# The output head of an S4 + recurrent-cell kernel: seven products for eight from stored row sums, two tiles at a time, with the state's term seeded in PSUM and the residual sum on GpSimd

## The chip, the cores and the metric

The kernel runs on one core of one Trainium2 chip. The metric is the device time of one execution in microseconds (us). Five engines work side by side: TensorE (PE, with its weight loads as PEld), VectorE (DVE), ScalarE (ACT), GpSimd (POOL) and SyncE (SP), which here only issues transfers. They synchronise by semaphores that the program writes out by hand.

## What is computed

Input x has 8 sequences of 2048 steps with 512 channels. A first layer normalises, convolves each channel with a long kernel and adds its normalised result back (the stored `x1`). The second layer normalises x1 to x2, runs a gated cell over 8 blocks of 2048 rows in 4 chains, and then applies the output head to every row:

```
for each of 8 steps:  f, i, g = gates(x2 @ W.T + c @ U.T + b);  c = f*c + i*g
h   = tanh(x2 @ wo.T + c_final @ uo.T + bo)
out = x1 + layernorm(h)
```

In the code the rows are cut in 128-row tiles. `unit_at(j, b)` is the block of 512 rows (4 tiles, `c` = 0 to 3) of sequence b at place j; c_final of a chain j is the state after b = 7, and its term c_final @ uo.T is shared by the eight units of that j. All matrix products are in two f16 parts with three terms (`PARTS`), so a product over 512 inputs is 12 matmuls of 128 inputs each.

## The kernel before, in words

1. **Setup and convolution** (to about 600 us). During 16 iterations `i` over groups of channels the weights are also scaled and split in f16 parts. The six gate weights are cut in seven quarter matrices, which are sums and differences of the four quarters of the weight; the two output weights (m = 6, 7) are only split (`wd`, `Wo`, `Uo`).
2. **Units** (`GROUPS` = 6 x 32 steps of one loop that every engine runs, to 2288 us). A unit is 512 rows. Its x2 and the state are held in seven combinations of quarter matrices, and a group (one gate, half of the outputs) is computed by seven products for eight: each of the products 1 to 7 is 256 columns wide and 6 matmuls deep for x2 and 6 for the state. Two banks, A and B, hold a group; banks go round by four groups. A group's products stand on PE in the order 4, 1, 3 (of the group before), 2, 5, 7 (of the group before), 6, and ACT and DVE copy and add between them. The turned x2 of a unit lies in `slot[u % 2]` in four parts; parts 0 and 1, the plain rows, are stored to DRAM (`xtd`, `store_xt`), since the head needs them again; x1 is stored too (`x1d`).
3. **The head** (2288 us to the end). For each j, `last_state(j)` multiplies the final state by Uo: 48 matmuls of 512 columns in four banks. DVE scales them and adds the bias, to `cu` in SBUF (L1739). Then 32 tiles `h` follow: PE makes 12 matmuls of 512 columns in one bank (L2061), DVE scales and adds `cu` (`head`, L1717), ACT takes the tanh (`head_tanh`, L1287), DVE its statistics (`head_stat`, L1724 and L1725), POOL works out scale and shift (L1015 to L1017), ACT applies them (`head_norm`, L1292), and DVE adds the residual x1 (`head_out`, L1730). SP stores the tile (L806), loads x1 tiles (`load_rb`, L782, eight buffers) and turned rows (`load_xt`, L776, two tiles each, six buffers).

The order of all this is written out by hand: each engine's program is a loop with fixed places, and a wait blocks all that stands behind it on its engine. `hv` is a chain: its instruction waits until the chain's last one has ended. The lines at which a tile's bank is released and the residual is added:

```
e.scalar_tensor_tensor(hp[h % NHP], bank[n % NB_][:, :], inv[3], cu[:, h % 4, :], MUL, ADD)
hv("hres").tensor_tensor(rb[h % NRB], hp[h % NHP], rb[h % NRB], ADD)
```

## Time and profile before

| | |
|---|---|
| median of 3 runs | 2673.97 us (2672.85 to 2675.7) |
| the profiled execution's own time | 2672.62 us |
| its span | 2670.8 us |
| TensorE busy | 2564.2 us, 96% |
| DVE, ACT, POOL busy | 1894.5, 1527.0, 1054.2 us |
| the head: from 2288.49 us to the last matmul's end | 372.97 us |
| last matmul's end to the span's end | 9.3 us |

The span is what the trace covers; the execution's own time is 1.8 us longer, and the median of the three runs 1.35 us above that. Busy shares are averages over stages with different limits, so the stage that the change rewrites has to be read alone. In a timeline a duration is from start to end of an instruction; the next may start on the same engine before that end, so the distance from start to start (here called pitch) is what an engine spends on it.

### The profile page before, as it was taken

The page shows a single profiled execution, that of the slowest core. Times are in us where ns is not written, and L with a number is a line of the kernel's source. Part 1 is how long each engine was busy: PE and PEld are TensorE (multiplying, and loading weights), DVE is VectorE, ACT ScalarE, POOL GpSimd, SP SyncE. Part 2 cuts the span into 40 slices and gives each one's busy share as a digit, 9 for nine tenths or more (in the row PEclk, how much of TensorE's full clock was granted, in tenths as well). Part 3 has the DMA queues.
Part 4 walks back from the last instruction along what each step waited for, and adds up shares of the span by engine and source line. Part 5 has one row for each costly group of instructions (what it writes and reads, how often), then busy time and mean ns, then how long its engine had stood idle before and what let it go on. Part 6 is the DMA issues. An engine that isn't in the chain of part 4 may idle for free.

```text
span 2670.8 us, 55058 instructions
## 1 busy us (share of the span) xinstructions
PE 2564.2 (96%) x21507; PEld 2093.8 (78%) x21507; DVE 1894.5 (71%) x3406; ACT 1527.0 (57%) x2864; POOL 1054.2 (39%) x1496
## 2 busy tenths in 40 slices
PE   5499999997999999999999999999999999999998
PEld 4278888886888888888888888888888888544443
DVE  8855656558886777667778877767777673678778
ACT  8656767567665555555556755555555553345444
POOL 7768687625232232222333523222222220245445
PEclk9799999998999999999999999999999999999999
DMA  8779787889644554355547564345544451478777
GB/s 357 280 237 313 265 298 273 288 292 309 151 138 111 126 132 105 98 119 126 132 99 169 156 157 117 99 104 127 138 104 100 113 120 70 167 264 306 260 256 260
DMA packets 510213, 489.95 MB, mean 183 GB/s; under 512 B 275584, under 2 KB 406912, under 8 KB 502656
## 3 DMA queue, kind: packets, MB, share of 16 engines
q1 hardware_dynamic: 509952, 486.43, 60.9%
q8 instruction: 169, 2.77, 0.4%
q14 instruction: 92, 0.75, 0.1%
HBM read 270.60 MB, written 150.73 MB: 158 GB/s over the span
## 4 chain that ended last, share of the span: by engine, by line
PE 89%; POOL 3%; DVE 2%; ACT 2%; DMA 2%; issue 1%; SPq 0%; POOLq 0%; DVEq 0%; ACTq 0%
PE bank L1987 31%; PE bank L1997 29%; PE bank L2061 12%; PE bank L1876 4%; PE bank L1826 3%; PE bank L1884 3%; PE bank L1862 3%; PE bank L1838 2%; PE bank L2045 2%; PE bank L1846 1%; POOL big L832 1%; POOL big L936 1%; DMA big<-big 1%; DMA yd<-big 0%; DVE big L1448 0%
## 5 line engine op out<-in xcount | busy, mean ns | idle before, releaser
L1987 PE MATMUL bank<-big 128*128 128x256 f16 x8064 | 1080.2, 274 | 17.2 <-DMA big<-big 7.8
L1997 PE MATMUL bank<-big 128*128 128x256 f16 x7056 | 962.6, 273 | 0.0
L1987 PEld LDWEIGHTS bank<-big 128*128 128x128 f16 x8064 | 790.9, 98 | 114.5 <-ACT big L1268 9.2
L1997 PEld LDWEIGHTS bank<-big 128*128 128x128 f16 x7056 | 690.4, 98 | 79.9
L977 POOL TENSOR_SCALAR big<-big 128x1 f32<-128x1 f32 x253 | 107.6, 425 | 1092.8 <-DVE big L1561 812.1
L2061 PE MATMUL bank<-big 128*128 128x512 f16 x1536 | 332.2, 379 | 0.0
L1228 ACT ACTIVATE big<-big 128x512 f32<-128x512 f32 x384 | 289.6, 803 | 14.1 <-DVE big L1705 14.1
L2061 PEld LDWEIGHTS bank<-big 128*128 128x128 f16 x1536 | 150.3, 98 | 181.2
L1705 DVE TENSOR_TENSOR big<-bank,big 128x512 f32<-128x512 f32 x192 | 130.7, 681 | 195.2 <-PE bank L1997 193.2
L1160 ACT ACTIVATE big<-big 128x512 f32<-128x512 f32 x256 | 206.1, 808 | 104.2 <-POOL big L979 100.6
L1187 ACT ACTIVATE big<-big 128x512 f16<-128x512 f32 x248 | 150.7, 623 | 118.2 <-DVE big L512 73.3
L1697 DVE TENSOR_TENSOR big<-bank,big 128x512 f32<-128x512 f32 x192 | 131.4, 684 | 110.1 <-PE bank L1997 108.9
L1438 DVE SCALAR_TENSOR_TENSOR big<-bank,big 128x320 f16<-128x320 f32 (+6 forms) x237 | 109.1, 460 | 138.9 <-ACT big L1072 137.2
L978 POOL TENSOR_TENSOR big<-big 128x1 f32<-128x1 f32 x253 | 193.3, 764 | 21.1
L1251 ACT ACTIVATE big<-bank 128x256 f32<-128x256 f32 x192 | 72.4, 377 | 220.6 <-PE bank L1997 213.2
L1287 ACT ACTIVATE big<-big 128x512 f32<-128x512 f32 x128 | 80.6, 629 | 199.1 <-DVE big L1717 199.1
L1268 ACT ACTIVATE big<-bank 128x512 f32<-128x512 f32 x192 | 113.1, 589 | 132.1 <-PE bank L1997 96.5
L1585 DVE TENSOR_TENSOR big<-big 128x512 f16<-128x512 f32 x248 | 168.7, 705 | 11.9 <-ACT big L1187 11.0
L918 POOL TENSOR_TENSOR big<-big 128x1024 f32<-128x1024 f32 x63 | 150.8, 2394 | 39.5 <-DMA big<-xg 39.3
L1826 PE MATMUL bank<-big 128*128 128x256 f32 x480 | 149.0, 393 | 15.0 <-DVE big L1420 10.4
L1876 PE MATMUL bank<-big 128*128 128x128 f32 x1024 | 159.2, 278 | 2.1 <-POOL big L929 2.1
L1279 ACT ACTIVATE big<-bank 128x256 f32<-128x256 f32 x192 | 72.2, 376 | 149.6 <-PE bank L1997 143.7
(226 smaller groups left out, 3718.9 us busy)
## 6 DMA issues: line engine op xcount, KB each, us to landing
big<-xr SPq DMA_DIRECT2D x16, 2048.0 KB, 8.8
big<-xg SPq DMA_DIRECT2D x64, 512.0 KB, 7.8
big<-kpad SPq DMA_DIRECT2D x32, 1024.0 KB, 12.1
yd<-big SPq DMA_DIRECT2D x16, 2048.0 KB, 16.9
big<-x SPq DMA_DIRECT2D x128, 256.0 KB, 3.2
x1d<-big SPq DMA_DIRECT2D x128, 256.0 KB, 2.0
xtd<-big SPq DMA_DIRECT2D x64, 512.0 KB, 4.6
big<-xtd SPq DMA_DIRECT2D x64, 512.0 KB, 4.1
```

Of the source, the lines that this page charges most:

```text
L918: e.tensor_tensor(ug, ug, st(0), SUB).then_inc(s["sub"], 1)
L978: rp().tensor_tensor(st[:, 7:8], st[:, 7:8], mhalf, ALU.pow).then_inc(s["rp"], 1)
L1160: return e.activation(o, rows.rearrange("p (g h) -> p g h", g=NG) if len(rows.shape) == 2 else rows, ACT.Identity, bias=st[:, 6:7], scale= ...
L1187: e.activation(xs16[k][:, 0, :].rearrange("p (g h) -> p g h", g=NG), source(i), ACT.Copy).then_inc(s["xh"], 1)
L1228: e.activation(zt[g][:, r::2, :], zt[g][:, r::2, :], ACT.Tanh if g == 2 else ACT.Sigmoid, bias=bs[:, g, a + 2 * r:a + 2 * r + 1], scale=in ...
L1585: e.tensor_tensor(lo, source(i), hi, SUB).then_inc(s["xlo"], 1)
L1697: e.tensor_tensor(z[:, 0:2, :], bank_b(n - 1)[:, :].rearrange("p (q t) -> p q t", q=2), z[:, 0:2, :], ADD).then_inc(s["u1"], 1)
L1826: ins = e.matmul(o, Gm, u[g % 3][:, k].rearrange("p h b -> p (h b)"), start=True, stop=(k == 0))
L1876: e.matmul(o, T[t % 3][:, h % 16, :], u[g % 3][:, :, h, :], start=(q == 0), stop=False, skip_group_check=True)
L1987: ins = e.matmul(o, WX[2 * g + lw][:, q, kt, 128 * a:128 * a + 128], slot[u % 2][:, part, lx, k0 + kt, :], start=(first and kt == 0 and (l ...
L1997: ins = e.matmul(o, WC[2 * g + lw][:, q, kt, 128 * a:128 * a + 128], cc[unit(u)[1] % 2][:, qc, lx, kt, :], start=False, stop=end, skip_gro ...
L2061: ins = e.matmul(bank[n % NB_][:, :], xt4[r % NXR][:, lx, kt, 128 * c:128 * c + 128], Wo[:, lw, kt, :], start=(a == 0), stop=(a == 11))
```

## The change

The head is no longer a loop of its own. It becomes 64 further steps (`PAIRS`, m = 0 to 63) of the units' loop, each for two tiles: tiles p and p + 2 of a 512-row block (p = m % 2). The roles are turned: the turned rows are the stationary side, and `wo`, now cut in seven quarters like the gates' weights (`Wq`), is the moving side, 256 columns wide. For this `store_xt` stores all four parts of a unit's turned rows (for 30 of the 32 units; the last two stay in `slot`), and `load_xu` loads seven eighths of them back for each two steps. `last_state` comes two steps ahead of each run of 16 steps (`LAST_AT`), the chains in the order j = 2, 3, 0, 1. DVE adds the bias to it (`head_state`) into blocks of SBUF; ACT copies two of these blocks (with zeros beside them) into the banks before a step's products (`head_seed`), and the other two are added by DVE where it moves products 6 and 5 out (`head_sixth`, `head_fifth`). ACT takes the tanh of 1024 elements. The rates of two tiles are worked out together on POOL, and the residual sum moves from DVE to POOL (`head_sum`), for all steps but the last one, which DVE adds in two halves.

The cut diff:

```diff
+JORDER = (2, 3, 0, 1)
+BORDER = (7, 0, 1, 2, 3, 4, 5, 6)
+LAST_AT = tuple(GROUPS + 16 * i - 2 for i in range(4))
+def place(n):
+    return n + 2 * sum(n >= a for a in LAST_AT)
+def head_unit(U):
+    return unit_at(JORDER[U // 8], BORDER[U % 8])
+LOADED = [U for U in range(NU) if U % 8 or U >= 16]
-NB_, NHP, NRB, NXR = 8, 6, 8, 6
+NZ, NRB, NXR = 5, 6, 4
...
             def store_xt(v):
-                for k in range(2):
-                    w.wait_ge(s[f"xq{k}"], 32 * v)
-                    e.dma_start(xtd[v, k], slot[v % 2][:, k].rearrange("p l k t -> p (l k t)")).then_inc(s[f"xs{k}"], 16)
+                for r in range(2):
+                    w.wait_ge(s[f"xq{2 * r}"], 32 * v)
+                    w.wait_ge(s[f"xq{2 * r + 1}"], 32 * v)
...
+            def load_xu(r):
+                U, k = LOADED[r], r % NXR
+                if r < 3:
+                    w.wait_ge(s["p7"], GROUPS - 2 + r)
                 else:
+                    w.wait_ge(s["p7"], GROUPS + 2 * (LOADED[r - NXR] if r >= NXR else 0) + 2)
...
-                    if i < 12 and i % 4 >= 2 and q == (0 if i == 2 else 0):
+                    if i % 4 >= 2 and q == 0:
                         quarter_sums(i)
...
+            def head_sum(m):
+                o = rb[m % NRB].rearrange("p r o -> p (r o)")
+                w.wait_ge(s["hn"], 2 * m + 2)
+                w.wait_ge(s[f"rb{m % NRB}"], 32 * (m // NRB) + 16)
+                e.tensor_tensor(o, zh[m % NZ].rearrange("p q t -> p (q t)"), o, ADD).then_inc(s["hres"], 1)
+            for m in range(PAIRS):
+                head_rates(m)
+                if m:
+                    head_sum(m - 1)
...
+            def head_seed(m):
+                n = GROUPS + m
+                i, p = m // 16, m % 2
+                w.wait_ge(s["u1"], place(n) - 3)
+                w.wait_ge(s["u2"], place(n) - 3)
+                if m % 16 < 2:
+                    w.wait_ge(s["u1"], place(LAST_AT[i]))
+                    w.wait_ge(s["u2"], place(LAST_AT[i]))
+                e.activation(bank_a(n)[:, :].rearrange("p (q t) -> p q t", q=2), two(cu_zero(i), cu_block(i, 2, p)), ACT.Copy).then_inc(s["pre"], 1)
+                e.activation(bank_b(n)[:, :].rearrange("p (q t) -> p q t", q=2), two(cu_block(i, 0, p), cu_zero(i)), ACT.Copy).then_inc(s["pre"], 1)
...
+            def head_sixth(m):
+                n, i, p = GROUPS + m, m // 16, m % 2
+                w.wait_ge(s["p6"], n + 1)
+                if m >= NZ:
+                    w.wait_ge(s["hres"], m - NZ + 1)
+                cu = f32(cu_block(i, 1, p), 256)
+                e.tensor_tensor(zh[m % NZ][:, 1, :], bank_a(n)[:, 0:256], cu, ADD).then_inc(s["k6"], 1)
...
+                        e.scalar_tensor_tensor(o, bo.rearrange("p (q t) -> p q t", q=2), scl[:, 1, 3:4], last_bank(i, r, p)[:, :].rearrange("p (q t) -> p q t", q=2),
+                                               MUL, ADD).then_inc(s[("u2", "u1")[r]], 1)
...
-                for a, (kt, lw, lx) in enumerate(TERMS):
-                    ins = e.matmul(bank[n % NB_][:, :], xt4[r % NXR][:, lx, kt, 128 * c:128 * c + 128], Wo[:, lw, kt, :], start=(a == 0), stop=(a == 11))
...
+            def head_product(m, k, o, sem=None):
+                U, p = divmod(m, 2)
+                q, part, k0, _ = PROD[k]
...
+                for kt in range(2):
+                    for lw, lx in PARTS:
...
+                        ins = e.matmul(o, xw, Wq[lw][:, q, kt, :], start=False, stop=(kt == 1 and (lw, lx) == PARTS[-1]), skip_group_check=True)
...
+            for n in range(TOTAL + 1):
+                if n in LAST_AT:
+                    last_state(LAST_AT.index(n))
                 if n < TOTAL:
                     A, Bn = bank_a(n), bank_b(n)
 
+                    if n >= GROUPS:
+                        w.wait_ge(s["pre"], 2 * (n - GROUPS) + 2)
+                    elif n >= 4:
+                        w.wait_ge(s["u2"], place(n) - 3)
+                    step(n, 4, A[:, 256:512], True)
+                    step(n, 1, A[:, 0:256], False, "pa")
```

How the order changes. On DVE, in the middle of the head, four instructions stood for one tile: the release of the bank, the two of the statistics, and the residual sum (bank numbers kept; s_ names are semaphores).

```order
L1717 SCALAR_TENSOR_TENSOR big<-bank4,big 128x512 [waits s_hd,s_hm]
L1724 BN_STATS big<-big 128x6 [waits s_hres,s_th]
L1725 BN_AGGR big<-big 128x2 [waits s_pr]
L1730 TENSOR_TENSOR big<-big 128x512 [waits s_hag,s_rb1,s_hn]
L1717 SCALAR_TENSOR_TENSOR big<-bank5,big 128x512 [waits s_hd,s_hm]
```

Now eight stand for two tiles, and at `LAST_AT` the state's four follow the second sum (L1804 is `head_sixth`, L1819 `head_fifth`, L1870 and L1884 the sums of banks B and A that also stand in the units' steps, L1844 `head_state`):

```order
L1804 TENSOR_TENSOR big<-bank6,big 128x256 [waits s_p6]
L1827 BN_STATS big<-big 128x6 [waits s_hag,s_hn,s_th]
L1828 BN_AGGR big<-big 128x2 [waits s_pr]
L1870 TENSOR_TENSOR big<-bank7,big 128x512 [waits s_k6,s_ka,s_p3]
L1827 BN_STATS big<-big 128x6 [waits s_hag]
L1828 BN_AGGR big<-big 128x2 [waits s_pr]
L1819 TENSOR_TENSOR big<-bank5,big 128x256 [waits s_hres,s_pb]
L1884 TENSOR_TENSOR big<-bank6,big 128x512 [waits s_k5,s_p7]
L1838 MEMSET big 128x256 [waits s_hag]
L1844 SCALAR_TENSOR_TENSOR big<-big,bank0 128x2x256 [waits s_ls,s_pr]
L1844 SCALAR_TENSOR_TENSOR big<-big,bank1 128x2x256 [waits s_ls]
```

Two more L1844 follow. The residual sum has left DVE, and no DVE instruction of a step reads two operands from SBUF.

On ACT, around the same place, a step is now: two normalisations (L1355), the tanh of a pair (L1343), the copy of products 4 and 1 (L1335), and the two seeds of the next step (L1322, L1323).

```order
L1335 ACTIVATE big<-bank2 128x2x256 [waits s_hres,s_pa]
L1322 ACTIVATE bank0<-big 128x512 [waits s_u2,s_u1]
L1323 ACTIVATE bank1<-big 128x512
L1355 ACTIVATE big<-big 128x512 [waits s_rhm] x2
L1343 ACTIVATE big<-big 128x1024
L1335 ACTIVATE big<-bank0 128x2x256 [waits s_hres,s_pa]
L1322 ACTIVATE bank2<-big 128x512 [waits s_u2,s_u1]
```

Before, ACT had a tanh and a normalisation of 512 elements for each tile, and nothing that PE waited for before its products. Here the seeds stand ahead of the normalisations, and they wait for the banks' sums.

On POOL, a step of the head before was L1015, L1016, L1017 for each tile. Now:

```order
L1073 TENSOR_SCALAR big<-big 128x2 [waits s_rhm,s_hag]
L1074 TENSOR_TENSOR big<-big 128x2 [waits s_rp]
L1076 TENSOR_SCALAR big<-big 128x1 [waits s_rp]
L1076 TENSOR_SCALAR big<-big 128x1 [waits s_rhm]
L1083 TENSOR_TENSOR big<-big 128x1024 [waits s_rb1,s_hn]
```

The 1024-wide sum of a pair stands behind the rates of the pair after it.

## Rows read from the trace of the kernel before

**Rows 1.** The chain of waits, 2150 to 2671 us: start us, us, what.

```profile
2277.36 0.66 PE bank L1997 x6
2288.49 10.36 PE bank L2045 x48
2298.85 82.88 PE bank L2061 x384
...
2578.57 82.89 PE bank L2061 x384
```

**Rows 2.** Groups by line and shape, 2280 to 2671 us.

```profile
L2061 PE MATMUL bank<-big 128*128 128x512 f16 x1536 | 332.2, 379 | 0.0
...
L1730 DVE TENSOR_TENSOR big<-big 128x512 f32<-128x512 f32 x128 | 88.6, 692 | 18.3 <-ACT big L1292 1.0 <-DVE big L1725 0.5
...
L1739 DVE SCALAR_TENSOR_TENSOR big<-bank,big 128x512 f32<-128x512 f32 x16 | 12.0, 751 | 17.5 <-PE bank L2045 17.1
```

**Rows 3.** Timeline of DVE, 2100 to 2125 us: start, us, engine, line, operation.

```profile
2113.55 0.42 DVE L514 TENSOR_TENSOR big<-big 128x256 f32<-128x256 f32 x1
2113.90 0.68 DVE L1568 TENSOR_TENSOR big<-big 128x512 f32<-128x512 f32 x1
2114.61 0.70 DVE L1569 BATCH_NORM_STATS2 big<-big 128x6 f32<-128x512 f32 x1
2115.34 0.18 DVE L1570 BATCH_NORM_AGGREGATE big<-big 128x2 f32<-128x6 f32 x1
2115.45 0.69 DVE L1585 TENSOR_TENSOR big<-big 128x512 f16<-128x512 f32 x1
2116.06 1.22 DVE L1661 TENSOR_TENSOR big<-big 128x1024 f32<-128x1024 f32 x1
```

**Rows 4.** Timeline of ACT, 2100 to 2130 us.

```profile
2106.19 0.60 ACT L1268 ACTIVATE big<-bank 128x512 f32<-128x512 f32 x1 [1.31 <-DVE big L1665]
2106.68 0.80 ACT L1160 ACTIVATE big<-big 128x512 f32<-128x512 f32 x1
2107.39 1.13 ACT L1187 ACTIVATE big<-big 128x512 f16<-128x512 f32 x2
```

**Rows 5.** Timeline of ACT, 2290 to 2312 us.

```profile
2292.85 1.06 ACT L1210 ACTIVATE big<-big 128x1024 f16<-128x1024 f32 x1 [2.02 <-DVE big L1643]
2293.82 0.61 ACT L1212 ACTIVATE big<-big 128x512 f16<-128x512 f32 x1
```

**Rows 6.** Groups of instructions by line and shape, POOL, 0 to 900 us.

```profile
L920 POOL TENSOR_TENSOR big<-big 128x1024 f32<-128x1024 f32 x63 | 151.0, 2396 | 4.9
...
L963 POOL TENSOR_TENSOR big<-big 128x512 f32<-128x512 f32 x24 | 30.5, 1270 | 61.5 <-DMA big<-wts 60.1
```

**Rows 7.** Timeline of POOL, 2305 to 2309 us.

```profile
2305.72 0.22 POOL L1015 TENSOR_SCALAR big<-big 128x1 f32<-128x1 f32 x1 [132.64 <-DVE big L1725]
2306.03 0.57 POOL L1016 TENSOR_TENSOR big<-big 128x1 f32<-128x1 f32 x1
2306.70 0.27 POOL L1017 TENSOR_SCALAR big<-big 128x1 f32<-128x1 f32 x1
```

**Rows 8.** Stretches of the span: DMA share and GB/s are the last columns.

```profile
2332.00:2342.00 10.00, 10.00 (x48) 4.54 (x47) 8.58 (x16) 4.99 (x9) 5.10 (x12) 1.00 1.03 390
...
2404.00:2475.00 71.00, 71.00 (x330) 32.20 (x329) 60.91 (x110) 36.75 (x55) 37.14 (x83) 1.00 0.90 307
```

**Rows 9.** Timeline of all engines, the last 16 us.

```profile
2666.71 0.81 ACT L1292 ACTIVATE big<-big 128x512 f32<-128x512 f32 x1 [1.19 <-POOL big L1017]
2667.56 0.69 DVE L1730 TENSOR_TENSOR big<-big 128x512 f32<-128x512 f32 x1 [1.01 <-ACT big L1292]
```

**Rows 10.** Timeline of all engines, 1524 to 1530 us.

```profile
1525.78 0.72 POOL L511 TENSOR_TENSOR big<-big 128x256 f32<-128x256 f32 x1
...
1525.96 2.23 DVE L1665 TENSOR_TENSOR big<-big 128x512 f32<-128x512 f32 x2 [0.20 <-ACT big L1228]
...
1526.58 1.06 POOL L512 TENSOR_TENSOR big<-big 128x256 f32<-128x256 f32 x1
```

More of the change, by code:

```diff
@@ L41 @@
 PARTS = [(0, 0), (0, 1), (1, 0)]
-TERMS = [(kt, lw, lx) for kt in range(4) for lw, lx in PARTS]
 class Engine:
@@ new lines, in sync_program @@
+            load_xu(0)
+            load_rb(0)
+            load_rb(1)
+            load_xu(1)
+            load_rb(2)
+            load_rb(3)
+            load_xu(2)
+            load_rb(4)
+            load_rb(5)
+            load_xu(3)
+            ready = NXR
+            for m in range(PAIRS):
+                U, p = divmod(m, 2)
+                b, j = unit(head_unit(U))
+                o = out[b, 512 * j:512 * j + 512, :].rearrange("(r p t) o -> p t r o", r=2, p=2)[p]
+                if m < PAIRS - 1:
+                    w.wait_ge(s["hres"], m + 1)
+                    e.dma_start(o, rb[m % NRB]).then_inc(s[f"rb{m % NRB}"], 16)
+                else:
+                    for r in range(2):
+                        w.wait_ge(s["hfin"], r + 1)
+                        e.dma_start(o[:, r], rb[m % NRB][:, r]).then_inc(s[f"rb{m % NRB}"], 16)
+                if m >= 2 and m + 4 < PAIRS:
+                    load_rb(m + 4)
+                if m in (6, 22):
+                    load_last((m - 6) // 16 + 2)
+                if m % 2 and ready < len(LOADED) and LOADED[ready - NXR] <= (m + 1) // 2:
+                    load_xu(ready)
+                    ready += 1
@@ L815, in sync_program @@
+            for k in range(NRB):
+                w.wait_ge(s[f"rb{k}"], 32 * len(range(k, PAIRS, NRB)) + (16 if k == (PAIRS - 1) % NRB else 0))
             w.wait_ge(s["wd"], stored(7))
@@ L1134, in act_program @@
                     for step, n, f in WEIGHTS_AT[i, j]:
-                        if step == "lo" and n < 12:
+                        if step == "lo" and n < 15:
                             m = 2 * (n // 4) + n % 2
@@ L1683, in dve_program @@
+            for n in range(TOTAL + 3):
                 u, gi = divmod(n, 6)
-                if u and 2 <= gi <= 4:
+                m = n - GROUPS
+                if 1 <= u <= NU and 2 <= gi <= 4:
                     state_sums(u - 1, gi - 2)
-                for step, v in DVE_AT[n, 0]:
-                    prepare(step, v)
+                if 0 <= m - 1 < PAIRS:
+                    head_sixth(m - 1)
+                if n < GROUPS + 6:
+                    for step, v in DVE_AT[n, 0]:
+                        prepare(step, v)
@@ L1699, in dve_program @@
                     new_state(n - 2)
-                for step, v in DVE_AT[n, 2]:
-                    prepare(step, v)
-                if 1 <= n <= GROUPS:
+                if 0 <= m - 2 < PAIRS:
+                    head_stat(m - 2, 1)
+                if 0 <= m < PAIRS:
+                    head_fifth(m)
+                if n < GROUPS + 6:
+                    for step, v in DVE_AT[n, 2]:
+                        prepare(step, v)
+                if 1 <= n <= TOTAL:
                     w.wait_ge(s["p7"], n)
+                    w.wait_ge(s["k5"], n)
@@ L1732, in dve_program @@
[L1732 to L1745 removed]
+                if n in LAST_AT:
+                    head_state(LAST_AT.index(n))
@@ L1748, in pe_program @@
+                if n < GROUPS + 6:
+                    for step, v in DVE_AT[n, 3]:
+                        prepare(step, v)
+            m = PAIRS - 1
+            w.wait_ge(s[f"rb{m % NRB}"], 32 * (m // NRB) + 16)
+            for r in range(2):
+                w.wait_ge(s["hn"], 2 * m + r + 1)
+                o = rb[m % NRB][:, r]
+                e.tensor_tensor(o, zh[m % NZ][:, 2 * r:2 * r + 2].rearrange("p q t -> p (q t)"), o, ADD).then_inc(s["hfin"], 1)
         def pe_program(e):
@@ new lines, in last_state @@
+                for p in range(2):
+                    slot_no = place(LAST_AT[i]) - 2 + p
+                    w.wait_ge(s["u1"], slot_no - 3)
+                    w.wait_ge(s["u2"], slot_no - 3)
+                    for r in range(2):
+                        for kt in range(4):
+                            q = ((0, 1), (3, 2))[r][kt // 2]
+                            for lw, lx in PARTS:
+                                ins = e.matmul(last_bank(i, r, p)[:, :], cc[j % 2][:, q, lx, kt % 2, 128 * p:128 * p + 128], Uo[:, lw, kt, :],
+                                               start=(kt == 0 and (lw, lx) == PARTS[0]), stop=(kt == 3 and (lw, lx) == PARTS[-1]))
+                                if kt == 3 and (lw, lx) == PARTS[-1]:
+                                    ins.then_inc(s["ls"], 1)
```

408 lines of the change are left out of this document (214 added, 194 removed).

## The prediction, made before the changed kernel ran

> **What bounds the kernel now.** I read the chain of waits first. In its last 520 us TensorE stands without a gap: the units' products follow each other at 0.66 us for 6 matmuls of 256 columns, and at 2288.49 us the head begins, four times a state block of 10.36 us (48 matmuls) and 82.88 us for 32 tiles (384 matmuls) [rows 1]. That is 215.8 ns for a matmul of 512 columns, 2.590 us for a tile, and 372.97 us to the last matmul at 2661.46 us; the span ends 9.3 us later. Other engines have slack there, so the head costs what PE issues, and fewer columns are time as long as every other engine keeps up. So I price one step of the new head on each engine from timelines, by pitch (start to start), and compare it with PE's.
>
> **TensorE.** Removed: 128 tiles of 12 matmuls of 512 columns, 1536 in all [rows 2], 128 x 2.590 = 331.5 us. Added: 64 steps of 7 products of 6 matmuls of 256 columns; a product is 0.655 us by the units' rhythm (17 products from 2277.36 to 2288.49 us [rows 1]), so a step is 4.587 us and all are 293.5 us. The state blocks stay, 41.4 us. Saving on PE: **38.0 us**, if nothing makes it wait.
>
> **VectorE, per step.** Pitches from [rows 3]: 256 elements 0.35 us (2113.55 to 2113.90); statistics 0.73 and 0.11, together 0.84; a 512-wide sum 0.61. A step has two of 256, two statistics, two sums of 512: 0.70 + 1.68 + 1.22 = 3.6 us of 4.587. The moved residual sum takes two times 0.69 us [rows 2] away from it. There is also a loop: the first statistic of a pair, sum B, the second statistic, `head_fifth` and sum A (0.84 + 0.61 + 0.84 + 0.35 + 0.69) come before the next pair's tanh, 1.06 us [rows 5], and its statistic waits for that. With two hops of 0.05 it is 4.49 us, just under PE's step. It fits with 0.1 us to spare.
>
> **ScalarE, per step.** Tanh of 1024: 0.97 [rows 5]; a copy out of a bank 0.49, a normalisation 0.71 (2106.68 to 2107.39) [rows 4]. The two seeds write PSUM from SBUF, an operation that the head of before does not have; the nearest rows are the copy the other way, 0.49, and the normalisation, 0.71. I take 0.5 each, since both are plain copies of 512. 0.97 + 0.49 + 1.0 + 1.42 = 3.9 us, at the upper bound 4.3. Hidden under PE either way.
>
> **GpSimd, per step.** The 1024-wide sum: 2.40 us for this size and type, or twice 1.27 for 512 [rows 6]; I take 2.4. The rates: 0.31 + 0.67 [rows 7] for one column; the power of two columns is taken 0.15 longer, and two last steps at 0.35. 1.83 + 2.42 = 4.25 us of 4.587, 93%. The moved sum more than doubles its work, and after PE it has the least room in plain work.
>
> **Transfers.** Per two steps: turned rows 1.835 MB (7 of 8 eighths of 2.1 MB), x1 1.05 MB, output 1.05 MB: 3.93 MB in 9.17 us, 429 GB/s inside a run, against 3.15 MB in 10.36 us now. The state blocks give PE 10.36 us per 16 steps in which it needs none of it: 31.5 + 1.05 MB per 83.8 us is 388 GB/s. What was reached with work queued is 390 GB/s for 10 us, with outputs among it [rows 8]; the mean of a run of the head is 307 GB/s at 90% of the queues' time [rows 8], but there PE paced it. Four buffers of turned rows let the loads run some 20 us ahead. So at 390 it is just enough: cost 0; if 307/0.90 = 341 GB/s is all there is, about 13 us (below). I take 2 us. A page of the Trainium skill, "DMA: Bandwidth & Descriptors", section "Where 436 GB/s comes from", says that for transfers between HBM and SBUF the HBM side binds at about 358 GB/s per core; by that figure a run's 32.5 MB take 91 us where PE needs 85, and the estimate would be a delay of up to 11 us in the last two runs, before the lead, rather than 2. The 390 GB/s of this trace stands against it.
>
> **Where a state block stands.** Now it is two steps ahead of a run, on PE, in the middle of the loop. The step after it cannot start its products before its two seeds, these wait for sum A of two steps before, and that for product 7, which PE only issues behind the state block: 3.93 us into the step, + 0.16 until the last matmul ends (379 against 216 ns [rows 2]), + 0.69 + 1.05 for two seeds and hops of 0.1 to 0.2 = 6.1 us, where PE could go on at 4.59. So **1.5 us, three times: 4.6**. `head_state` on DVE, 4 x 0.75 us [rows 2], stands behind that same sum A and delays DVE's next step to 7.6 us; the slack of its loop and of the fifth product's wait (1.7 us) takes that. For the first state block PE is in the units' steps of 9.17 us, with room; but in the first three steps ACT and DVE still finish the last unit's gates and state beside the head's work. I take 2 us (0 to 4).
>
> **The end.** Now: 9.3 us after the last matmul, of which 2.55 are behind the last sum's end (2668.25 to 2670.8 [rows 9]). Then: about 2.4 us after PE's end DVE has the statistics of pair 62, and POOL does in order its rates (1.9), the sum of pair 61 (2.4), the rates of pair 63 in two halves (2.6) and the sum of pair 62 (2.4): 11.7 us. Behind it 1.05 MB goes out: 2.55 + 2.0 for the larger amount. 16.2 us, **6.9 more than now**.
>
> **The rest.** The output weight cut in seven instead of split: 4 more sums on POOL (1.27 each [rows 6]), some ten copies on ACT, in a convolution iteration in which earlier gates have the same; hidden by PE, and 0 to 2 us if not. Stores of turned rows double, 1 MB more in each unit of 55 us, 2.7 us of the queues at 390 GB/s. Each is issued one landing later, and behind it on SP stand the x1 stores of the next unit; covered by DVE's work in the steady units. In the first two units the queues are full and PE waits anyway: 0 to 3 us. I take 1 us for both.
>
> **The sum:** -38.0 + 4.6 + 2 (start) + 2 (transfers) + 6.9 + 1 = -21.5 us. Against the profiled execution's own 2672.6 us that gives 2651.1; the median of the runs stands 1.35 us above it, so **2652.5 us**. The spread of the estimates (start 0 to 4, transitions 0 to 2.5 each, rest 0 to 5) gives 2646 to 2657.
>
> **Rivals.** *(B) Transfers pace the head.* At 341 GB/s two steps take 11.5 us of the queues' time, eight of these and the state's load 95 us, where PE with its waits needs 85. The last two runs lose 10 us each, the first two, where one unit is not loaded, 4.6 each: 29 us less the lead of the buffers and what is fetched before the first step (16): 13 us, so 2664. For it: the 90% share now. Against it: 390 GB/s in [rows 8] with a share of 1.03, when a backlog had built up. The page named above is this rival's rule; the trace does not agree with it. Chance 0.20.
>
> *(C) GpSimd held up by DVE: slower than before.* When DVE adds two SBUF operands, POOL's sum of 256 takes 1.06 us instead of 0.72, and DVE's two sums of 512 take 2.23 us [rows 10] where one is 0.69 [rows 3]. If the 1024-wide sum is stretched like that (2.4 x 1.47 = 3.5), POOL's step is 5.4 us. It can lag 2.5 us before ACT and the five `zh` buffers wait for it; each run then loses 16 x 0.8 - 2.5 = 10 us, four 40 us: about 2692. It decides from a sum of 3.2 us on (a step of 5.08, where the 21.5 us are gone). Against it: in the convolution stage, where DVE's work reads PSUM with one SBUF operand, the 1024-wide op is 2396 ns on the mean of 63 [rows 6], and the order of the new step has only such DVE work. The Trainium skill's "GPSIMD Engine Reference", section "Key points", names just two SBUF inputs or a two-port mode as what contends; by it this rival needs the statistics to run in such a mode. Chance 0.08.
>
> *(D) The loops are a little longer than their rows.* Every engine is within 2 to 22% of PE's step, and the DVE and ACT loop within 2%. If hops and seeds add 0.2 us to it, a step is 4.7 us, 64 x 0.1 = 7 us; with 0.4 us, 19 us: 2657 to 2671. Nothing in the rows asks for it, but 0.1 us is the whole margin. Chance 0.10.
>
> **How the numbers follow.** My case has 0.62, B 0.20, D 0.10, C 0.08. The predicted time is that of my case. A measurement tells apart some 0.2%, 5.3 us: faster is below 2668.6. Faster: 0.62 + 0.20 + 0.04 of D = 0.86; same: the rest of D, 0.06; slower: C, 0.08. For the range I go to the bound of B and most of D, 2669, and below to 2645, where start and transitions cost nothing.
>
> **What would show it.** PE's head as runs of steps at 4.59 us, with a gap of 1.5 us one step behind each of three state blocks; the PE time from the first state block to the end of the last product without the two units' steps near 343 us. The 1024-wide POOL sum at 2.4 us: at 3.2 or more (C) holds. PE waits put down to a transfer of turned rows, and GB/s flat near 340 to 360 in the last two runs, mean (B); waits on ACT's seeds or DVE's `head_fifth` in every step mean (D). The tail would be 16 us, with POOL's sum in the chain. The forecast is wrong if the steps are longer than 4.7 us, or if the gain is lost before 2270 us, in the units.

## The result, and the profile after

The changed kernel takes **2650.12 us** (median of 4 runs, 2649.85 to 2650.23), the kernel before 2673.74 (4 runs beside it, 2672.85 to 2675.7). The ratio is 0.9910, 95% interval 0.9898 to 0.9922: 23.6 us less, where 21.5 were forecast. The profiled execution has a span of 2648.6 us.

Page of the kernel after, sections 1 and 2 (the 40 slices are 66.2 us each; the head begins in the sixth from the end):

```profile
PE 2526.6 (95%) x22659; PEld 2205.2 (83%) x22659; DVE 1841.0 (70%) x3413; ACT 1623.0 (61%) x3003; POOL 1133.2 (43%) x1437
...
GB/s 355 286 227 312 267 314 270 271 293 343 181 196 116 130 139 167 119 116 131 141 167 150 204 152 143 166 116 116 135 137 168 119 82 49 168 333 362 370 359 321
```

TensorE's timeline from the first state block on (start, us, engine, line; L2169 is `last_state`, L2194 `head_product`; in brackets the idle time ahead of a row and what ended it). It answers to [rows 1]:

```profile
2270.39 10.52 PE L2169 MATMUL bank<-big 128*128 128x512 f16 x48
...
2304.33 8.68 PE L2194 MATMUL bank<-big 128*128 128x256 f16 x78
2313.32 51.92 PE L2194 MATMUL bank<-big 128*128 128x256 f16 x474 [0.31 <-DVE big L1804]
2365.07 10.52 PE L2169 MATMUL bank<-big 128*128 128x512 f16 x48
2375.43 4.75 PE L2194 MATMUL bank<-big 128*128 128x256 f16 x42
2381.52 68.95 PE L2194 MATMUL bank<-big 128*128 128x256 f16 x630 [1.34 <-ACT bank L1323]
2450.31 10.52 PE L2169 MATMUL bank<-big 128*128 128x512 f16 x48
2460.67 4.75 PE L2194 MATMUL bank<-big 128*128 128x256 f16 x42
2466.75 68.95 PE L2194 MATMUL bank<-big 128*128 128x256 f16 x630 [1.34 <-ACT bank L1323]
2535.54 10.52 PE L2169 MATMUL bank<-big 128*128 128x512 f16 x48
2545.90 4.75 PE L2194 MATMUL bank<-big 128*128 128x256 f16 x42
2551.99 79.72 PE L2194 MATMUL bank<-big 128*128 128x256 f16 x726 [1.34 <-ACT bank L1323]
```

The head is runs of steps without a gap: 630 matmuls are 15 steps and take 68.79 us to the next block (2450.31 - 2381.52), 4.586 us a step. One step behind each of three state blocks stands the same gap: the step from 2375.43 is issued by 2380.02, the next begins at 2381.52, 1.50 us later. TensorE has no wait for a transfer in the head. All that it waited for there is four waits, in two lines of its view of waits (us in total, times, longest; the engine's idle time, which is 0.16 us a wait less than the gap from start to start):

```profile
PE bank L2194 <- ACT bank L1323: 4.0, 3, 1.3
PE bank L2194 <- DVE big L1804: 0.3, 1, 0.3
```

**The balance of the two executions** (2670.8 and 2648.6 us, -22.2). In TensorE's timeline of the kernel before, the first state block stands here:

```profile
2288.33 10.52 PE L2045 MATMUL bank<-big 128*128 128x512 f16 x48
```

(The 2288.49 of [rows 1] is the same block in the chain of waits, where the end of the product before it comes off.) The change puts the first state block ahead of 20.96 us of units' products (18.34 before 2299.09, 2.62 among the first head steps); without the block the units would end at 2270.39 + 20.96 = 2291.35 us, against 2288.33 before: +3.0. From there to TensorE's end at 2631.71 are 340.4 us, against 373.1: -32.8. Behind it 16.9 us are left, against 9.3: +7.5.

A step of the middle of the head, DVE's and POOL's timelines. They answer to [rows 3], [rows 6] and [rows 7]:

```profile
2499.75 0.41 DVE L1804 TENSOR_TENSOR big<-bank,big 128x256 f32<-128x256 f32 x1
2501.11 0.69 DVE L1827 BATCH_NORM_STATS2 big<-big 128x6 f32<-128x512 f32 x1 [0.94 <-ACT big L1343]
2501.84 0.18 DVE L1828 BATCH_NORM_AGGREGATE big<-big 128x2 f32<-128x6 f32 x1
2501.95 0.69 DVE L1870 TENSOR_TENSOR big<-bank,big 128x512 f32<-128x512 f32 x1
2502.55 0.68 DVE L1827 BATCH_NORM_STATS2 big<-big 128x6 f32<-128x512 f32 x1
2503.27 0.18 DVE L1828 BATCH_NORM_AGGREGATE big<-big 128x2 f32<-128x6 f32 x1
2503.37 0.41 DVE L1819 TENSOR_TENSOR big<-bank,big 128x256 f32<-128x256 f32 x1
2503.69 0.68 DVE L1884 TENSOR_TENSOR big<-bank,big 128x512 f32<-128x512 f32 x1
2504.29 0.41 DVE L1804 TENSOR_TENSOR big<-bank,big 128x256 f32<-128x256 f32 x1
```

```profile
2503.55 0.23 POOL L1073 TENSOR_SCALAR big<-big 128x2 f32<-128x2 f32 x1 [0.47 <-DVE big L1828]
2503.86 0.71 POOL L1074 TENSOR_TENSOR big<-big 128x2 f32<-128x2 f32 x1
2504.67 0.62 POOL L1076 TENSOR_SCALAR big<-big 128x1 f32<-128x1 f32 x2
2505.26 2.36 POOL L1083 TENSOR_TENSOR big<-big 128x1024 f32<-128x1024 f32 x1
```

DVE's step is 4.54 us (2499.75 to 2504.29), of which 0.94 is the wait for tanh. So its loop goes at its own pace, behind the delay of a state block, and gains 0.04 us a step on TensorE's 4.586: it is that much short of being the bound. POOL's 1024-wide sum is 2.37 us, not held up; it waits 0.47 us in a step.

The end, POOL from the last rates on, and DVE's last sum; it answers to [rows 9]:

```profile
2634.21 0.23 POOL L1073 TENSOR_SCALAR big<-big 128x2 f32<-128x2 f32 x1 [0.48 <-DVE big L1828]
...
2635.91 2.34 POOL L1083 TENSOR_TENSOR big<-big 128x1024 f32<-128x1024 f32 x1
2638.34 0.23 POOL L1073 TENSOR_SCALAR big<-big 128x1 f32<-128x1 f32 x1
...
2641.34 2.34 POOL L1083 TENSOR_TENSOR big<-big 128x1024 f32<-128x1024 f32 x1
```

```profile
2642.26 1.97 DVE L1896 TENSOR_TENSOR big<-big 128x512 f32<-128x512 f32 x1 [1.01 <-ACT big L1355]
```

The rates of the last pair stand behind a sum that nobody needs so early, and DVE's last 512-wide sum takes 1.97 us instead of 0.69, as long as POOL's last sum is under way beside it (until 2643.68) and 0.55 more, to 2644.23.

### The profile page after: what moved, and what is told of

Same layout as the page of the kernel before. It is cut to its first block, busy times and chain, and to the rows that moved or that the text cites. A ratio compares the mean times of both kernels' runs of the same rounds, so it can differ in the third digit from the quotient of the medians.

```text
span 2648.6 us, 57574 instructions
## 1 busy us (share of the span) xinstructions
PE 2526.6 (95%) x22659; PEld 2205.2 (83%) x22659; DVE 1841.0 (70%) x3413; ACT 1623.0 (61%) x3003; POOL 1133.2 (43%) x1437
## 4 chain that ended last, share of the span: by engine, by line
PE 84%; DVE 4%; POOL 4%; ACT 3%; DMA 3%; issue 2%; SPq 1%; DVEq 0%; POOLq 0%; ACTq 0%
PE bank L2138 31%; PE bank L2148 29%; PE bank L2194 8%; PE bank L2027 4%; PE bank L1977 3%; PE bank L2013 3%; PE bank L2035 2%; PE bank L1989 2%; PE bank L2169 2%; DVE big L1827 1%; PE bank L1997 1%; ACT big L1343 1%; POOL big L886 1%; POOL big L990 1%; DVE big L1884 1%
## 5 line engine op out<-in xcount | busy, mean ns | idle before, releaser
L2138 PE MATMUL bank<-big 128*128 128x256 f16 x8064 | 1078.8, 273 | 20.8 <-ACT big L1387 8.3
L2148 PE MATMUL bank<-big 128*128 128x256 f16 x7056 | 962.5, 273 | 0.0
L2138 PEld LDWEIGHTS bank<-big 128*128 128x128 f16 x8064 | 790.4, 98 | 117.4 <-ACT big L1387 9.9
L2148 PEld LDWEIGHTS bank<-big 128*128 128x128 f16 x7056 | 690.4, 98 | 79.9
L1884 DVE TENSOR_TENSOR big<-bank,big 128x512 f32<-128x512 f32 x256 | 175.1, 684 | 197.1 <-PE bank L2148 195.0
L2194 PE MATMUL bank<-big 128*128 128x256 f16 x2688 | 295.3, 273 | 4.4 <-ACT bank L1323 4.0
L1299 ACT ACTIVATE big<-big 128x512 f32<-128x512 f32 x384 | 289.6, 803 | 13.5 <-DVE big L1884 13.4
L2194 PEld LDWEIGHTS bank<-big 128*128 128x128 f16 x2688 | 262.4, 98 | 37.0 <-ACT bank L1323 4.9
L1870 DVE TENSOR_TENSOR big<-bank,big 128x512 f32<-128x512 f32 x256 | 176.3, 689 | 140.9 <-PE bank L2148 118.5
L1231 ACT ACTIVATE big<-big 128x512 f32<-128x512 f32 x256 | 205.9, 808 | 100.3 <-POOL big L1033 96.5
L1719 DVE TENSOR_TENSOR big<-big 128x1024 f16<-128x1024 f32 (+1 forms) x180 | 133.8, 786 | 29.6 <-ACT big L1281 29.6
```

The lines of the kernel that those rows point to most:

```text
L1231: return e.activation(o, rows.rearrange("p (g h) -> p g h", g=NG) if len(rows.shape) == 2 else rows, ACT.Identity, bias=st[:, 6:7], scale= ...
L1299: e.activation(zt[g][:, r::2, :], zt[g][:, r::2, :], ACT.Tanh if g == 2 else ACT.Sigmoid, bias=bs[:, g, a + 2 * r:a + 2 * r + 1], scale=in ...
L1870: e.tensor_tensor(z[:, 0:2, :], bank_b(n - 1)[:, :].rearrange("p (q t) -> p q t", q=2), z[:, 0:2, :], ADD).then_inc(s["u1"], 1)
L1884: e.tensor_tensor(z[:, 2:4, :], bank_a(n - 1)[:, 0:256].unsqueeze(1).to_broadcast([128, 2, 256]), z[:, 2:4, :], ADD).then_inc(s["u2"], 1)
L2138: ins = e.matmul(o, WX[2 * g + lw][:, q, kt, 128 * a:128 * a + 128], slot[u % 2][:, part, lx, k0 + kt, :], start=(first and kt == 0 and (l ...
L2148: ins = e.matmul(o, WC[2 * g + lw][:, q, kt, 128 * a:128 * a + 128], cc[unit(u)[1] % 2][:, qc, lx, kt, :], start=False, stop=end, skip_gro ...
```

## The experiments

The lines of code shift by a few in the experiments, so a row is told here by its operation. Times of different chips are compared by their ratio to the kernel before on the same chip.

**The change again, beside the next three.**

> The changed kernel itself, for comparison on the same chip: 2650 us, 23.6 below the kernel before.

Measured: 2649.46 us (2648.83 to 2651.5) against 2674.46 before, ratio 0.9909 (0.9894 to 0.9924). The next three are read against this.

**The gap behind a state block.** Each of the last three state blocks is cut in halves of 24 matmuls, with products 3 and 7 of the step before between them. On DVE (not in this cut) sum A and the four `head_state` are put ahead of `head_fifth` in that step:

```diff
-                if n in LAST_AT:
+                early = n in LAST_AT[1:]
+                if early:
+                    last_state(LAST_AT.index(n), (0,))
+                    w.wait_ge(s["k5"], n)
+                    step(n - 1, 3, bank_b(n - 1)[:, 256:512], False, "p3")
+                    w.wait_ge(s["k6"], n)
+                    step(n - 1, 7, bank_a(n - 1)[:, 0:256], False, "p7")
+                    last_state(LAST_AT.index(n), (1,))
```

> The last three state blocks are cut in two halves on TensorE, and products 3 and 7 of the step before are issued between the halves; DVE makes sum A and the state's four ahead of the fifth product's move there. If the 1.5 us gap behind each state block is the wait for seeds, which hang on sum A and that on product 7 (my step), the three gaps close: 4.5 us less, 2645.6. If the gap comes from the freshly started bank, or DVE's four state instructions hold the next step, the gaps stay or move one step on: 2649 to 2651.

Measured: 2644.45 us (2644.21 to 2647.17), ratio 0.9891 (0.9877 to 0.9906): 5.0 us less than the change beside it. TensorE's timeline of this kernel at the second block:

```profile
2366.57 5.34 PE L2171 MATMUL bank<-big 128*128 128x512 f16 x24
2371.75 1.47 PE L2196 MATMUL bank<-big 128*128 128x256 f16 x12
2373.06 5.34 PE L2171 MATMUL bank<-big 128*128 128x512 f16 x24
2378.24 72.21 PE L2196 MATMUL bank<-big 128*128 128x256 f16 x660
```

The 660 matmuls behind the block have no gap. So the chain that the prediction gave for it (the seeds wait for sum A, this for product 7, and that was issued behind the block) is the cause: the bank is as freshly started and DVE's four `head_state` stand there as before, and the gap is gone all the same. The three gaps were 4.5 us, and the other 0.5 lies within the spread.

**The end.** The residual sums of the last three pairs stand on DVE, behind its last statistics (`ON_DVE` = 3):

```diff
-                if m:
+                if 0 < m <= PAIRS - ON_DVE:
                     head_sum(m - 1)
```

> The residual sums of pairs 61 and 62 go to DVE, which is idle by then, as that of pair 63 has. If GpSimd's queue of rates and sums sets the end (my step, 16.2 us forecast), the tail falls from 16.9 to about 13 us: 3.9 us less, 2646.2. If the last transfers set it, it stays within 1 us.

Measured: 2646.19 us (2645.47 to 2647.12), ratio 0.9896 (0.9881 to 0.9911), 3.3 us less than the change. TensorE ends at 2632.08, 13.4 us before the end instead of 16.9: 3.5 us of the 3.9 expected, and what is missing is less than the spread. There is a hold-up at this end, on DVE's and POOL's timelines of this kernel:

```profile
2636.82 2.34 DVE L1899 TENSOR_TENSOR big<-big 128x1024 f32<-128x1024 f32 x2
```

```profile
2636.81 1.65 POOL L1078 TENSOR_TENSOR big<-big 128x1 f32<-128x1 f32 x1
...
2639.77 0.57 POOL L1078 TENSOR_TENSOR big<-big 128x1 f32<-128x1 f32 x1
```

The same power of one column (`L1078`, the second of a pair's rates) takes 1.65 us beside DVE's two sums of 1024 and 0.57 after them. It ends at 2638.46, behind the first sum and beside the second, so it seems to get its turn between the two; the two starts are 0.01 us apart, too near to say from the trace who came first.

**The units, 3 us later.** The first two units don't store parts 2 and 3 of their turned rows, and the head reads those of unit 2 in their place (so their output is another one):

```diff
+                    if r and v < 2:
+                        e.dma_start(xtd[v][:, 2, 0, 0, 0:64], slot[v % 2][:, 0, 0, 0, 0:64]).then_inc(s[f"xs{r}"], 16)
+                        continue
```

> Parts 2 and 3 of the turned rows of units 0 and 1 are not stored (64 columns in their place), and the head reads those of unit 2 for them, so the output of these two units is of wrong inputs. If the doubled stores in the first two units, where the queues are full, cost the 2 us that TensorE is behind between 600 and 700 us, they come back: 2648.1. If the loss is the seventh quarter matrix or the layout elsewhere, nothing changes.

Measured: 2649.07 us (2648.42 to 2650.31), ratio 0.9906 (0.9889 to 0.9922). Taking these stores away gives nothing back that could be told from the spread. Its timeline shows two limits close together: TensorE begins the units' first product of the state at 691.00 us, ahead of the change (692.37), but just before that it waits 1.66 us for a transfer, a wait that the change does not have, and at the wait behind it the two are level again, 721.28 and 721.26.

**The residual sum back on DVE.** It stands at the end of a step, where DVE would wait for tanh:

```diff
-                if m:
-                    head_sum(m - 1)
...
+                if 0 <= m - 4 < PAIRS - 1:
...
+                    e.tensor_tensor(o, zh[k % NZ].rearrange("p q t -> p (q t)"), o, ADD).then_inc(s["hres"], 1)
```

> The change with one part undone: the 1024-wide residual sum of pair m-4 stands on VectorE again, as the last thing of a step (63 of them; the last one stays halved as it is). Theory 1 (what VectorE frees is what the saving stands on, both by plain work and by the loop of tanh, statistics and sums): the sum takes 2 x 0.69 = 1.38 us or, as in the run with the end's sums on VectorE, 2.34 us; VectorE has 3.6 us of 4.587 in a step and waits about 1.0 us for tanh. At 1.38 a step is 0.4 us over, 4.75 to 5.0 us, and 63 steps give +10 to +26 us; at 2.34 it is about 5.9 us and +85 us, far slower than the change. Theory 2 (the wait for tanh hides the sum): steps stay at 4.59, time within 3 us of the change. GpSimd's busy time falls by 149 us in either.

Measured: 2651.84 us (2650.87 to 2652.89) against 2675.32, ratio 0.9913 (0.9898 to 0.9927): the time of the change. But not because the wait hid the sum. Groups of DVE and POOL, 2400 to 2600 us of this kernel (busy us, mean ns, idle before):

```profile
L1825 DVE BATCH_NORM_STATS2 big<-big 128x6 f32<-128x512 f32 x76 | 52.1, 685 | 0.0
L1857 DVE TENSOR_TENSOR big<-big 128x1024 f32<-128x1024 f32 x38 | 46.2, 1216 | 4.7 <-ACT big L1353 4.7
```

```profile
L1076 POOL TENSOR_SCALAR big<-big 128x1 f32<-128x1 f32 x76 | 55.5, 731 | 7.3
```

DVE's wait for tanh is gone, its step is full, and from block to block (16 steps) TensorE takes 86.1 us (2365.41, 2451.54, 2537.62 us) where the change has 85.2. Its first block begins at 2270.37, as in the change (2270.39), and TensorE ends at 2635.96 instead of 2631.71: 4.3 us lost in the steps. The end is 13.4 us instead of 16.9, since a sum on DVE is half as long as on POOL: 3.5 us given back. Theory 1 was right about the mechanism and wrong about the price: 1.13 us by pitch for 1024 elements, not twice 0.69, so the step is 4.64 and not 4.75 or more. [Rows 3] had that price, in its last line, 1.22 us. POOL's product of one column (L1076, the shift, the last of a pair's rates), 731 ns on the mean instead of 265, pays for it beside DVE's sum, in time that POOL has. So against a sum at this place of DVE's step, moving it to POOL bought 4.3 us in the steps and cost 3.5 at the end.

**Two SBUF operands on DVE, beside POOL (rival C).** One 512-wide maximum is added on DVE in 60 steps, its result read by nothing. First it stands where DVE would wait for tanh, with both operands in SBUF as below, or with `bank_a(n - 1)[:, 256:512]` as one of them:

```diff
+                if 4 <= m < PAIRS:
+                    w.wait_ge(s["p6"], n)
...
+                    e.tensor_tensor(f32(x1_at + 7168, 512), f32(win_at + 2816, 512), f32(x1_at + 7168, 512), MAX).then_inc(s["spare"], 1)
                 if 0 <= m - 1 < PAIRS:
                     head_sixth(m - 1)
```

> The change with one operation of VectorE added in 60 steps: a maximum of 512 elements whose two operands both stand in SBUF, issued where VectorE would wait for tanh (its result is read by nothing). It pairs with the next run, where one operand comes from PSUM. Theory C (two SBUF operands on VectorE hold GpSimd up): GpSimd's 1024-wide sum takes 2.9 to 3.5 us on the mean instead of 2.37, or its rates are stretched, and with a step of 4.25 us before, GpSimd reaches 4.8 us or more: steps 4.7 to 5.1 us, +5 to +30 us. Rival: GpSimd's durations stay within 5%, the 0.6 us lie in VectorE's wait for tanh, and the time is that of the change within 3 us.

> The same added operation of VectorE, 512 elements in the same place of 60 steps, but with one operand read from PSUM. Theory C expects GpSimd's 1024-wide sum to stay at 2.37 us and the time within 3 us of the change, since 0.61 us fit into the wait of about 1.0 us for tanh; what is above that is plain length of VectorE's queue and no contention. Rival (any VectorE work slows GpSimd): GpSimd's sum is stretched as in the run before.

Measured: 2653.55 us (2651.3 to 2654.14), ratio 0.9917, and 2651.29 us (2650.52 to 2652.08), ratio 0.9910. Both lie in the wait for tanh, which shrinks from 0.94 to 0.34 us. POOL's sum is 2389 and 2371 ns, the product of one column (L1076) 354 and 265. That is a hold-up of 0.09 us on a small operation, and none that this pair could show for the sum: DVE's operation had no POOL sum beside it. So it was put where it has one, between the first statistic of a pair and the sum of the second bank, which is also inside the loop (the PSUM operand is now `bank_b(n - 1)`):

```diff
                     w.wait_ge(s["k6"], n)
+                    if 4 <= m < PAIRS:
...
+                        e.tensor_tensor(f32(x1_at + 7168, 512), f32(win_at + 2816, 512), f32(x1_at + 7168, 512), MAX).then_inc(s["spare"], 1)
                     z = zt[(n - 1) % 3] if n <= GROUPS else zh[(m - 1) % NZ]
```

> The change with one operation of VectorE added in 60 steps, 512 elements with one operand from PSUM, this time inside the loop that goes from tanh over the statistics and sums to the next tanh: between the first statistic of a pair and the sum of the second bank. It is under way while GpSimd does its 1024-wide sum. Theory (the loop, 4.545 us by the last run's steps of the trace of the change, is the next bound right behind TensorE's 4.586): a step is 4.545 + 0.60 = 5.15 us and the time rises by 60 x 0.56 = 34 us; GpSimd's sum stays at 2.37 us. Rival: VectorE has about 1.0 us to spare in a step, the 0.60 us lie in it, and the time is that of the change within 3 us.

> The same operation in the same place, but with both operands from SBUF. Theory 1 (VectorE's operation on two SBUF operands and GpSimd's exclude each other for their whole length, whoever comes second waits): it comes 3.1 us after the second statistic, GpSimd's 1024-wide sum runs from 1.9 to 4.25 us after it, so VectorE's operation lasts about 1.1 us longer than 0.68, and a step is 5.15 + 1.1 = 6.3 us: about +100 us, with GpSimd's sum still at 2.4 us. Theory 2 (rival C of the prediction: GpSimd is the one held up): its sum is 2.37 + 0.7 = 3.05 us or more, VectorE's operation stays 0.68, and the time is that of the run before within 5 us, since GpSimd has 4.25 + 0.7 us of work in a step of 5.15. Theory 3 (no contention in this pair): both durations stay and so does the time.

Measured, one run each, against 2673.91 before (the change is 2650 there by its ratio): 2684.93 us with one operand from PSUM, **+35**; 2733.54 us with both from SBUF, **+84**. TensorE's timeline with the PSUM operand:

```profile
2502.75 4.82 PE L2198 MATMUL bank<-big 128*128 128x256 f16 x42 [0.39 <-DVE big L1819]
2507.96 4.81 PE L2198 MATMUL bank<-big 128*128 128x256 f16 x42 [0.39 <-DVE big L1819]
```

A step is 5.21 us, where 5.15 was worked out, and TensorE waits for `head_fifth` (L1819) in 51 of them, 21.8 us in all. DVE has 0.94 us of waiting in each step, and still 0.60 us put into the step at this place goes to the time almost in full. It is the length of the loop that counts, not DVE's share. With both operands from SBUF, DVE and POOL:

```profile
2506.13 1.02 DVE L1872 TENSOR_TENSOR big<-big 128x512 f32<-128x512 f32 x1
...
2512.02 1.27 DVE L1872 TENSOR_TENSOR big<-big 128x512 f32<-128x512 f32 x1
```

```profile
2504.23 2.37 POOL L1083 TENSOR_TENSOR big<-big 128x1024 f32<-128x1024 f32 x1 [1.81 <-ACT big L1355]
...
2510.37 2.37 POOL L1083 TENSOR_TENSOR big<-big 128x1024 f32<-128x1024 f32 x1
```

DVE's operation ends at 2507.15 and 2513.29, both times 0.55 us after POOL's sum (2506.60 and 2512.74). So POOL, which came first, isn't touched (mean 2365 ns), and DVE waits for its end (mean 1525 ns of the 31 from 2400 to 2600 us, against 682 in the wait for tanh, where it had no sum beside it). Theory 1 holds. The steps between blocks are 6.13 us (2421.22 to 2427.35 us on TensorE) instead of the 6.3 worked out, since DVE's operation is 0.93 us longer there (1610 ns, the median of the 60) and not 1.1. Sixty such steps would cost 93 us, but TensorE waits for `head_fifth` in only 52 (68.7 us in all): while TensorE does a state block DVE's loop can catch up, and in the first steps of every run there is no wait for it. Rival C's direction is refuted for this pair: the long sum that came first isn't held up.

**What the transfers can give (rival B).** Each output pair is stored once more, to a scratch tensor, 0.52 MB a step:

```diff
+                    e.dma_start(exd[m], rb[m % NRB].rearrange("p r o -> p (r o)")).then_inc(s[f"ex{m % NRB}"], 16)
```

> The change, and each output pair is stored a second time, to a scratch tensor in HBM: 0.52 MB more in each of 63 steps, in rows of 4 KB. A run of 16 steps then moves 32.5 + 8.4 = 40.9 MB. It measures what the transfers can give when they pace the head. Theory 1 (390 GB/s, the stretch of the trace of before): a run takes 105 us where the products need 85 with the state block; less the lead of the buffers, about +60 us, and GB/s flat at 390 in the head. Theory B (341 GB/s): 120 us a run, about +120 us, flat at 341. PE's waits are then put down to transfers in both.

Measured: 2695.14 us (one run), 44 us more than the change by its ratio. Stretches of this kernel, and of the change (the last two columns are DMA share and GB/s):

```profile
2480.00:2550.00 70.00, 58.88 (x504) 50.29 (x502) 45.84 (x101) 51.42 (x74) 47.33 (x64) 0.95 1.03 414
```

```profile
2365.00:2450.00 85.00, 83.66 (x721) 70.17 (x719) 59.85 (x134) 65.43 (x96) 60.94 (x81) 1.00 0.95 363
2560.00:2625.00 65.00, 65.00 (x598) 58.26 (x596) 50.78 (x116) 58.42 (x87) 54.19 (x71) 1.00 1.02 397
```

With TensorE waiting for turned rows (26.4 us in 12 waits), the transfers run flat at **414 GB/s**; from block to block are 93.3 and 101.8 us instead of 85.2. The waits are not the whole price. Behind six of the seven waits of 2.7 us or more the next 84 matmuls take 10.7 to 11.0 us instead of 9.33, at a granted clock of 0.84 to 0.87 over that stretch, so a part of it was at the lower of the two levels (1.2 instead of 2.4 GHz); behind the five waits of 1.2 to 1.5 us the clock is 1.00. That is 9.3 us more, and 4.8 us more stand behind TensorE's end. Neither of the two capacities of the expectation was right; 390 was nearer. The change's run of 32.5 MB needs 79 us at 414 where TensorE takes 85. It moves 363 GB/s in the second run and 397 in the last, behind the last block. That is 4% below 414, but the share of the queues' time, 1.02, is almost that of the bound stretch, 1.03, and its packets are smaller (28% of the bytes in packets of 2 KB, 21% with the extra stores). How much there was to spare in the last run is therefore not shown; TensorE did not wait for it.

**The residual sum alone, in the kernel before.**

```diff
-                hv("hres").tensor_tensor(rb[h % NRB], hp[h % NHP], rb[h % NRB], ADD).then_inc(s["hres"], 1)
+                e.tensor_tensor(rb[h % NRB], hp[h % NHP], rb[h % NRB], ADD).then_inc(s["hres"], 1)
...
+                if h:
+                    head_out(h - 1)
```

> The kernel before, with one part of the change alone: the residual sum of a tile, 512 elements, stands on GpSimd behind the rates of the tile after it. The theory (TensorE sets the old head's pace, 2.59 us for a tile): VectorE loses 0.69 us a tile that it had in hand anyway; GpSimd has 1.3 us of rates and 1.27 us of sum, 2.6 us, no room at all. The time is that of the kernel before, 0 to 5 us more (a tile of 2.6 to 2.63 us, and an end about 1 us longer). Rival (VectorE's two SBUF operands had held GpSimd up in the old head, and moving them frees it): faster by up to 5 us.

Measured: 2674.07 us (10 runs, 2672.7 to 2675.98), ratio 1.0001 (0.9992 to 1.001). TensorE has 82.88 us from the first tile of a block to the next block, as before; POOL takes 1272 ns for a sum, and its tile (0.22 + 0.57 + 0.26 + 1.27 us with the spaces between) fills the 2.59 us. This part is worth nothing alone, and as the run with the sum back on DVE shows, almost nothing net in the change either. The gain is TensorE's columns.

**Both that gained, together.**

> The two parts that gained alone, together: the product that the seeds of the second step wait for stands between two halves of a state block, and the residual sums of the last three pairs stand on VectorE. Alone they gave 5.0 and 3.3 us against the change on the same chip. They lie in different places (three transitions, the end), so the theory is that they add: 8 us, 2641.5 us and a ratio to the kernel before of 0.988. Rival: without the three waits the loop (4.545 us) or the transfers, 4 us less behind, take the gain back in the last run, and the time is 2644 or more.

Measured: **2641.42 us** (2640.67 to 2642.97), ratio 0.9880 (0.9864 to 0.9897), faster than both kernels: 32.5 us below the kernel before, some 8.3 below the change by its ratio. They add. TensorE's last block and last run:

```profile
2531.41 5.34 PE L2181 MATMUL bank<-big 128*128 128x512 f16 x24
2536.59 1.48 PE L2206 MATMUL bank<-big 128*128 128x256 f16 x12
2537.90 5.34 PE L2181 MATMUL bank<-big 128*128 128x512 f16 x24
2543.08 82.86 PE L2206 MATMUL bank<-big 128*128 128x256 f16 x756
```

In the head TensorE waits for 0.3 us in all, and 13.4 us are left behind it.

## Why the prediction was right

TensorE's columns and the three transitions came as worked out. That the total is off by no more than 1 us (-22.2 against -21.5 between the two profiled executions) is in part luck: start and transfers were 3.5 us too dear and the end and the rest 2.6 us too cheap.

**TensorE, 38.0 us.** Right. The head without its gaps is 340.4 - 5.0 = 335.4 us against 373.1: 37.7 us.

**The three transitions, 4.6 us.** Right in size (1.50 each) and in cause: the split block took them away.

**The start, 2 us (0 to 4).** 0.5: one wait of 0.31 us for DVE's `head_sixth`. ACT and DVE had room beside the last unit.

**Transfers, 2 us.** 0. The step of the argument that failed is the capacity: "at 390 it is just enough" took the fastest stretch seen as what can be had. The transfers give 414 GB/s when work is queued. Rival B, 341 GB/s, is out, and so is, as a bound for this kernel on one core, the about 358 that the prediction cites from the Trainium skill's "DMA: Bandwidth & Descriptors". The Trainium skill's "HBM Reference", section "Specifications (TRN2)", gives this as the share of a core when both of a pair stream, and about 425 for one alone; by that figure the estimate would have been 0. The 414 measured here is 3% below it.

**The end, +6.9 us.** +7.5. POOL's order (rates, sum, rates in two halves, sum) came as written, 2.34 us a sum. POOL's last sum ends 11.97 us after TensorE, where 11.7 were worked out. What the working did not have: DVE's last sum of two SBUF operands waits for it and ends 0.55 us later (left alone, 0.69 us long, it would have been done at 2642.95, ahead of POOL's). Behind that stand 4.4 us, where 4.55 were taken.

**The loop, 4.49 us.** 4.54: tanh of 1024 takes 1.15 us and not 1.06, and DVE's pieces with the hops came 0.04 shorter. The margin was 0.04 us and not 0.1. Rival D had the place right, and the 35 us for 0.60 us per step show how near it was: the change stands that close to an edge. (Its price had a slip: 7 us on top of 2652.5 is 2659.5, not 2657.)

**Plain work.** DVE 3.60 us a step (4.54 less 0.94 of waiting), as forecast; POOL 4.07 (4.54 less 0.47), 4.25 forecast. A seed, 0.5 us in the sum, is 0.52 by pitch.

**The rest, 1 us.** 3.0 in the pair of profiled executions, and this is the one term that stays open. The kernel before with only its sum on POOL has the same units, yet its first state block begins at 2290.56, not 2288.33: 2.2 us are spread between executions of the same code. The first block of the change and its variants begins between 2269.30 and 2271.89 in twelve executions (mean 2270.6, this one 2270.39). That puts the loss at 1 to 3 us. The traces show where it lies: the units' first product of the state begins at 689.35 us in the kernel before, at 691.60 in the one with only its sum on POOL, and between 691.00 and 693.81 (mean 692.5) in the twelve; 1400 us later, at 2091.18, 2093.41 and 2094.45 on the mean, the distances are the same within 0.2 us. So the steady units lose nothing, and all of it is lost ahead of some 690 us. Taking the doubled stores of the first two units away did not give it back; the seventh quarter of the output weight wasn't tried, so the cause stays open.

**Rival C.** It had the pair of operations right and the victim wrong. [Rows 10] showed both engines stretched, and the prediction read from it a stretch for POOL. The runs show no stretch but a turn: whoever comes second waits until the other has ended. [Rows 10] fit this too: DVE's two sums end at 1528.19, again 0.55 us behind POOL's (1527.64). The rule of the Trainium skill's "SBUF — State Buffer", section "SBUF: two separate sides", says just this, an exclusive lock held for the whole instruction, for a DVE operation with two SBUF inputs against a GpSimd operation that reads SBUF. The rows here agree with it (1525 and 682 ns for DVE's 512-wide operation, beside POOL's sum and away from it). So the question is not how much DVE work there is, but which two operations meet.

## What to carry to other kernels

Price a loop by its length and its place, apart from the shares of its engines: DVE waited 0.94 us in each step of 4.59, and 0.60 us put into the loop cost 35 us, while the same 0.60 us put into the wait cost nothing. When a long block is put into the pipeline of one engine, ask which product behind it feeds the wait of the step after next, and cut the block there. A move that evens the engines' shares can be worth little or nothing in the steady state (4.3 us here, 0 in the kernel before) and still cost at the end (3.5 us), where the slower engine's operations stand in the chain one by one; there the order can be another than in the loop.

## What the runs showed of the hardware

- DVE and POOL exclude each other for whole operations when DVE reads two SBUF operands: DVE's 512-wide one takes 1525 ns on the mean beside POOL's 1024-wide sum and 682 without; POOL's power of one column takes 1.65 us beside two DVE sums of 1024 and 0.57 after them, its product of one column 731 ns on the mean beside one such sum and 265 without. With one operand of DVE's from PSUM, or statistics, neither is touched (POOL's sum 2369 ns, DVE 691).
- The transfers of one core gave 414 GB/s for 70 us, in packets mostly of 2 to 8 KB, loads and stores mixed, with a share of 1.03; 390 GB/s in [rows 8] was not the limit.
- A sum of 1024 elements of fp32 from two SBUF operands takes 1.22 us on DVE (1.13 by pitch) and 2.37 on POOL.
